# Causal attention in a fused vision kernel: the products for q as four tensor tiles of 32 rows by 32 columns

## The chip, the cores and the metric

The program runs on one NeuronCore of a Trainium2 chip. The metric is the device time of one execution in microseconds. The core has a matrix engine (PE, TensorE), a vector engine (DVE), a scalar engine (ACT), GpSimd (POOL) and queues of DMAs issued from SyncE (SP). Each engine takes its instructions in program order and waits on semaphores. Matmul results go to PSUM, which has eight banks of 512 float32 columns on each of 128 partitions.

## The reference, cut to what matters

Four layers follow each other on the same activations, 16 images of 56 x 56 = 3136 tokens with 32 channels: a window attention, two token MLPs, and twice (L2, L3) a causal attention over all 3136 tokens of an image with an expert-choice layer behind it. The change touches only the two causal attentions:

```
Q = embeddings @ W_Q
K = embeddings @ W_K
V = embeddings @ W_V
scores = jnp.einsum('bqd,bkd->bqk', Q, K) * scale
masked = jnp.where(causal[None, :, :], scores, -inf)
probs = jax.nn.softmax(masked, axis=-1)
return jnp.einsum('bqk,bkd->bqd', probs, V)
```

The kernel folds the weights together: with x the normalised tokens, the scores are x (W_Q W_K^T) x^T, so that one small matrix A (32 x 32) is enough. "q" below is A^T x^T, and the normalised tokens themselves serve as keys. What is computed and all sizes stay the same in the changed kernel.

## The kernel before, in words

`causal_attention` handles the images one after the other. Of each image it first makes VT (line 208, 32 channels of the transposed tokens, replicated four times over the 128 partitions, so that each group of 32 partitions holds a copy) and QT_ (line 209, the same for q). The replication has a purpose: a matmul that contracts over 32 channels uses only 32 rows of the array, and each copy feeds another group of 32 rows.

- **Scores** (line 404): keys on the output's partitions, 512 queries as columns. They are tiles of 32 rows by 128 columns and alternate between row groups 0 and 1 (`g0 = C * (n % 2)`, line 401). ACT takes the exponential from PSUM (line 529).
- **Maxima** (line 425): queries on the partitions, up to 512 keys as columns, in row groups 2 and 3 (line 422). DVE reduces each bank to one maximum for each query (line 561). The negated maxima go by DMA (line 289) into a row of QT_, as the channel that subtracts them from the scores.
- **pv** (line 502): exponentials times values, as four column tiles (128 rows by 32 columns), in batches of about 10 to 12 score banks; mask preloads (line 414), transposes that make VT (line 455) and the final product of a query block (lines 475 and 479) use all 128 rows.
- **q** (line 463): a stationary operand of 32 rows by 128 columns, A replicated four times (`A`, line 217), on row group 0, over 512 columns of VT (64 for the last of the seven blocks of an image). The result fills all 128 partitions of one bank, and ACT copies it to QT_ (line 546). An image has seven of these products; those of image i+1 stand within the work of image i.

Every float32 matmul appears in the trace as two passes, each with its own LDWEIGHTS and MATMUL. All work goes through one ring of eight PSUM banks (`RING`, line 80): `bank_free` (line 375) makes a matmul wait until ACT or DVE has read what was in the bank eight entries before. The order is a list `WORK` (line 172), sorted by a planned time and a rank, the same for all engines. It fixes where each q stands; scores and maxima go into the list mostly as two scores and two maxima in turn.

A line number with three forms (L404, L425, L502 and so on) names the same kind of work in both layers; the tiles are called L2a_... and L3a_.... In both the seven q of an image stand in the same places.

Of the kernel before, what the change touches and what calls it, by code (L numbers as in the profile page):

```python
# [21 lines left out]
C = 32  # L22
# [49 lines left out]
def causal_attention(nc, m, k, wq, wk, wv, eps, tag):  # L72

    NB = m.NB
    QB = 512
    NJ = -(-S // QB)
    QT = QB // P
# [5 lines left out]
    def rows(t):  # L83
        return P if t < LT else LAST
# [107 lines left out]
    with ExitStack() as ctx:  # L192
        def sb(name, shape, dt=F32):
            return ctx.enter_context(nc.sbuf_tensor(f"{tag}_{name}", shape, dt))
# [13 lines left out]
        VT = sb("vT", [P, 2, S])  # L208
# [8 lines left out]
        A = sb("A", [C, QT, C])  # L217
# [6 lines left out]
        def bank_of(x):  # L224
            if x[0] == "acc":
                x = ("pv", *x[1:])
            return R[PLACE[("mask", x[1]) if x[0] == "max" and x[1] in MASK_AT else x] % RING]
# [47 lines left out]
        item_full, item_copied, ot_ready = sem("item_full"), sem("item_copied"), sem("ot_ready")  # L275
        acc_copied, acc_added, rd_ready, t_added = sem("acc_copied"), sem("acc_added"), sem("rd_ready"), sem("t_added")

        with nc.Block() as block:
# [95 lines left out]
            def _(pe):  # L374
# [17 lines left out]
                for x in WORK:  # L392
                    kind = x[0]
                    if kind == "score":
                        n = x[1]
                        img, j, bank = SCORES[n]
                        bank_free(x)
                        if n == score_at(img, j):

                            pe.wait_ge(shift_in, shifts(img, j))  # L400
                        g0 = C * (n % 2)
                        for u, c0, c1, o in bank:
                            r = rows(u)
                            last = nc.tensor.matmul(bank_of(x)[0:r, o:o + c1 - c0],  # L404
                                                    VT[g0:g0 + C, img % 2, u * P:u * P + r],
                                                    QT_[g0:g0 + C, img % 2, j * QB + c0:j * QB + c1],
                                                    start=True, stop=True)
                        last.then_inc(s_full, 1)
                    elif kind == "mask":

                        _, j, _ = MAXES[x[1]]
                        bank_free(x)
                        mask = k.mask_qk[:][:, None, :].to_broadcast([P, QT, P]) if j < TAIL else k.mask_qk[:, P - LAST:P]
                        nc.tensor.matmul(bank_of(x)[:, 0:width(j)], k.ident_bf[:], mask, start=True, stop=False)
                    elif kind == "max":
                        n = x[1]
                        img, j, (part, d) = MAXES[n]
                        if n not in MASK_AT:
                            bank_free(x)
                        if n == max_at(img, j):  # L420
                            pe.wait_ge(item_copied, COPIED[("q", img, j)] + 1)
                        g0 = C * (2 + n % 2)

                        def dots(o, q0, c0, c1, start=True, stop=True):
                            return nc.tensor.matmul(bank_of(x)[:, o:o + c1 - c0], QT_[g0:g0 + C, img % 2, q0:q0 + P],  # L425
                                                    VT[g0:g0 + C, img % 2, c0:c1], start=start, stop=stop)

                        q0 = j * QB if j < TAIL else S - P
                        if part == "edge" and j < TAIL:

                            for i in range(QT):
                                last = dots(i * P, q0 + i * P, q0 + i * P, q0 + (i + 1) * P, False, i == QT - 1)
                        elif part == "edge":
                            last = dots(0, q0, LT * P, S, False)
                        elif part == "near":

                            if d == 0:
                                dots(0, q0 + P, q0, q0 + P)
                                last = dots(P, q0 + 3 * P, q0, q0 + 3 * P)
                            else:  # L440
                                last = dots(0, q0 + 2 * P, q0, q0 + 2 * P)
                        elif part == "far":
                            last = dots(0, q0 + d // j * P, d % j * QB, d % j * QB + QB)
                        else:
                            last = dots(0, q0, d * QB, d * QB + QB)
                        last.then_inc(m_full, 1)
                    elif kind == "vT":
                        _, img, f = x
                        bank_free(x)
                        if f == 0:  # L450
                            pe.wait_ge(vr_ready, img + 1)
                        for i in range(q_tiles(f)):
                            t = QT * f + i
                            r = rows(t)
                            last = nc.tensor.transpose(bank_of(x)[:, i * P:i * P + r],
                                                       VR[0:r, t].rearrange("p a c -> p (a c)"), k.ident[0:r, 0:r])
                        last.then_inc(item_full, 1)
                    elif kind == "q":
                        _, img, f = x
                        w = width(f)  # L460
                        bank_free(x)
                        pe.wait_ge(item_copied, COPIED[("vT", img, f)] + 1)
                        nc.tensor.matmul(bank_of(x)[:, 0:w], A[:].rearrange("p r c -> p (r c)"),
                                         VT[0:C, img % 2, f * QB:f * QB + w],
                                         start=True, stop=True).then_inc(item_full, 1)
                    elif kind == "final":
                        _, img, j = x
                        bank_free(x)
                        pe.wait_ge(acc_copied, FINAL[x] + 1)
                        added = [n for y, n in ADD.items() if y[:2] == (img, j)]  # L470
                        if added:
                            pe.wait_ge(acc_added, added[-1] + 1)
                        if j < TAIL:

                            nc.tensor.matmul(bank_of(x)[:, 0:QT * (C + 1)], O[:, FINAL[x] % 2],
                                             WFB[:].rearrange("p q c -> p (q c)"),
                                             start=True, stop=True).then_inc(item_full, 1)
                        else:
                            nc.tensor.matmul(bank_of(x)[0:LAST, 0:C + 1], O[:, FINAL[x] % 2, 0:LAST], WF[:],
                                             start=True, stop=True).then_inc(item_full, 1)  # L480
                    elif kind == "pv":
                        _, img, j, n0, n1 = x
                        bank = bank_of(x)
                        bank_free(x)
                        pe.wait_ge(exp_done, n1)
                        masked = [n for n in range(n0, n1) if n in MASK]
                        if masked:
                            pe.wait_ge(mask_done, MASK[masked[-1]] + 1)
                        if n0 == score_at(img, j):
                            pe.wait_ge(v_ready, img + 1)  # L490
                        order = [(u, c0) for n in range(n0, n1) for u, c0, *_ in SCORES[n][2]]
                        for n in range(n0, n1):
                            for u, c0, c1, o in SCORES[n][2]:
                                r = rows(u)

                                if j < TAIL:
                                    cuts = [(i, i * P - c0, (i + 1) * P - c0, [y for y, c in order if c <= i * P])
                                            for i in range(c0 // P, QT)]
                                else:
                                    cuts = [(u % 4, 0, LAST, [y for y, c in order if y % 4 == u % 4])]  # L500
                                for i, a, b, same in cuts:
                                    last = nc.tensor.matmul(bank[C * i:C * i + C, 0:b - a], V[0:r, img % 2, u, :],  # L502
                                                            E[0:r, n % RE, o + a:o + b],
                                                            start=u == same[0], stop=u == same[-1])
                            last.then_inc(pv_done, 1)
# [1454 lines left out]
```

## Time and profile before

| what | value |
|---|---|
| median of 2 runs | 4702.2 us (4697.58 to 4706.83) |
| the profiled execution: time | 4710.27 us |
| the profiled execution: span of its instructions | 4708.6 us |
| PE busy | 4141.0 us (88%), 51290 matmul passes |
| DVE busy | 3134.4 us (67%) |
| ACT busy | 2752.3 us (58%) |
| POOL busy | 1430.2 us (30%) |
| mean granted TensorE clock | 0.942 of 2.4 GHz |

The busy time of an engine is the union of its records. A record of a matmul starts when its weights begin to load or its columns begin to stream, and its end is modelled: it includes the way through the array. So several matmuls in different row groups lie above each other in the trace, and a PE that is "busy" may well have three of its four row groups free. The causal attentions take the stretches from 1550 to 2885 us (L2) and from 3130 to 4450 us (L3).

### The profile page before, as it was taken

The numbers are of one execution on the slowest core, as the hardware profiler recorded it, in microseconds if no ns is written. First come the engines' busy times: TensorE is split into PE (matmuls) and PEld (weight loads), VectorE is DVE, ScalarE is ACT, GpSimd is POOL, SyncE is SP. The second block draws the span as 40 slices with busy tenths as digits, with TensorE's granted clock in tenths as the row PEclk, the third lists the DMA queues.
The fourth block names the chain that finished last, engine by engine and source line by source line (L and its number), as shares of the span: only waits on it lengthen the run. The fifth ranks groups of instructions, "written<-read, shape, count | busy, mean of one in ns | idle before, by whom it ended". The sixth has DMA issues, their size and how long they took to land. (4 is left out here: it accounts for less than half of the span.)

```text
span 4708.6 us, 125775 instructions
## 1 busy us (share of the span) xinstructions
PE 4141.0 (88%) x51290; PEld 2867.8 (61%) x51290; DVE 3134.4 (67%) x6164; ACT 2752.3 (58%) x5706; POOL 1430.2 (30%) x2222
## 2 busy tenths in 40 slices
PE   3888888888686799999999999779999999999975
PEld 2666666666332466666676666456666666666754
DVE  4777777777798466666666666536666666666653
ACT  2777777776586355655655555415555556556541
POOL 4333223321000343433433432122433434334220
PEclk9999999999798699999999999769999999999987
DMA  1200000000000000000000000000000000000003
GB/s 25 33 3 3 2 2 3 2 2 2 3 1 1 1 2 2 2 2 3 2 3 2 2 2 2 6 1 2 2 2 2 3 2 2 2 2 2 3 6 55
DMA packets 348272, 24.07 MB, mean 5 GB/s; under 512 B 346388, under 2 KB 347700, under 8 KB 347700
## 3 DMA queue, kind: packets, MB, share of 16 engines
q1 hardware_dynamic: 347700, 16.03, 4.7%
q8 instruction: 409, 6.70, 0.6%
q14 instruction: 163, 1.34, 0.1%
HBM read 7.88 MB, written 6.42 MB: 3 GB/s over the span
## 5 line engine op out<-in xcount | busy, mean ns | idle before, releaser
L561 DVE TENSOR_REDUCE L2a_mx<-L2a_r 128x1 f32<-128x512 f32 (+4 forms) x1344 | 760.8, 627 | 243.4 <-PE L2a_r L425 240.3
L561 DVE TENSOR_REDUCE L3a_mx<-L3a_r 128x1 f32<-128x512 f32 (+4 forms) x1344 | 760.5, 627 | 239.8 <-PE L3a_r L425 236.4
L529 ACT ACTIVATE L2a_e<-L2a_r 128x512 f32<-128x512 f32 (+3 forms) x1344 | 658.8, 579 | 284.9 <-PE L2a_r L404 282.7
L529 ACT ACTIVATE L3a_e<-L3a_r 128x512 f32<-128x512 f32 (+3 forms) x1344 | 658.6, 579 | 280.5 <-PE L3a_r L404 278.5
L425 PE MATMUL L2a_r<-L2a_vT,L2a_qT 32*128 32x512 f32 (+3 forms) x3488 | 817.6, 529 | 0.0
L425 PE MATMUL L3a_r<-L3a_vT,L3a_qT 32*128 32x512 f32 (+3 forms) x3488 | 815.0, 528 | 0.1
L404 PE MATMUL L2a_r<-L2a_qT,L2a_vT 32*128 32x512 f32 (+4 forms) x3488 | 779.8, 518 | 29.4 <-DMA L2a_qT<-L2a_nm 29.4
L404 PE MATMUL L3a_r<-L3a_qT,L3a_vT 32*128 32x512 f32 (+4 forms) x3488 | 777.6, 516 | 27.3 <-DMA L3a_qT<-L3a_nm 27.3
L1454 POOL TENSOR_SCALAR win_xw<-win_xr,win_mv,win_rs 32x343 f32<-32x343 f32 (+7 forms) x432 | 327.9, 779 | 703.3 <-ACT win_rs L1242 703.2
L404 PEld LDWEIGHTS L2a_r<-L2a_qT,L2a_vT 32*128 32x128 f32 x3488 | 372.1, 188 | 189.3 <-issue 100.3
L404 PEld LDWEIGHTS L3a_r<-L3a_qT,L3a_vT 32*128 32x128 f32 x3488 | 370.6, 187 | 186.8 <-issue 98.9
L425 PEld LDWEIGHTS L2a_r<-L2a_vT,L2a_qT 32*128 32x128 f32 x3488 | 394.0, 194 | 51.0 <-DVE L2a_mx L561 24.3
L425 PEld LDWEIGHTS L3a_r<-L3a_vT,L3a_qT 32*128 32x128 f32 x3488 | 390.8, 192 | 51.0 <-DVE L3a_mx L561 25.0
L502 PEld LDWEIGHTS L2a_r<-L2a_e,L2a_v 128*32 128x32 f32 x10400 | 302.5, 111 | 118.9 <-ACT L2a_e L529 100.3
L502 PEld LDWEIGHTS L3a_r<-L3a_e,L3a_v 128*32 128x32 f32 x10400 | 302.3, 111 | 119.1 <-ACT L3a_e L529 100.3
L502 PE MATMUL L2a_r<-L2a_e,L2a_v 128*32 128x128 f32 x10400 | 347.1, 273 | 3.9 <-POOL L2a_e L363 3.1
L502 PE MATMUL L3a_r<-L3a_e,L3a_v 128*32 128x128 f32 x10400 | 346.5, 273 | 4.1 <-POOL L3a_e L363 3.3
L1106 PE MATMUL win_mx<-win_mk,win_xw 113*64 113x196 f32 x2048 | 202.7, 339 | 134.1 <-issue 126.5
L1268 ACT COPY win_yb<-win_yp 64x512 f32<-64x512 f32 x256 | 148.3, 579 | 237.5 <-PE win_yp L1190 236.0
L1220 ACT COPY win_mq<-win_pq 32x392 f32<-32x392 f32 x512 | 246.6, 482 | 57.3 <-PE win_pk L1099 50.1
L363 POOL TENSOR_SCALAR_AFFINE_SELECT L2a_e<-L2a_e 128x128 f32<-128x128 f32 (+2 forms) x304 | 98.8, 326 | 581.2 <-ACT L2a_e L529 567.5
L363 POOL TENSOR_SCALAR_AFFINE_SELECT L3a_e<-L3a_e 128x128 f32<-128x128 f32 (+2 forms) x304 | 98.8, 326 | 576.8 <-ACT L3a_e L529 563.0
(370 smaller groups left out, 6745.0 us busy)
## 6 DMA issues: line engine op xcount, KB each, us to landing
L2a_qT<-L2a_nm SPq DMA_DIRECT2D x768, 0.5 KB, 2.0
L3a_qT<-L3a_nm SPq DMA_DIRECT2D x768, 0.5 KB, 2.0
T<-in_x SPq DMA_DIRECT2D x16, 384.0 KB, 3.7
out<-T SPq DMA_DIRECT2D x16, 384.0 KB, 4.0
win_mq<-win_nmt SPq DMA_DIRECT2D x256, 3.1 KB, 1.7
win_msk<-in_L_conv_pos_emb SPq DMA_DIRECT2D x49, 0.2 KB
L2a_qT<-L2a_nm SPq DMA_DIRECT2D x32, 0.2 KB, 1.8
L3a_qT<-L3a_nm SPq DMA_DIRECT2D x32, 0.2 KB, 1.8
```

Of the source, the lines that this page charges most:

```text
L363: nc.gpsimd.affine_select(out=e, in_=e, compare_op=ALU.is_ge, fill=0.0, base=0, pattern=pattern, channel_multiplier=-1).then_inc(mask_done, 1)
L404: last = nc.tensor.matmul(bank_of(x)[0:r, o:o + c1 - c0], VT[g0:g0 + C, img % 2, u * P:u * P + r], QT_[g0:g0 + C, img % 2, j * QB + c0:j * ...
L425: return nc.tensor.matmul(bank_of(x)[:, o:o + c1 - c0], QT_[g0:g0 + C, img % 2, q0:q0 + P], VT[g0:g0 + C, img % 2, c0:c1], start=start, st ...
L502: last = nc.tensor.matmul(bank[C * i:C * i + C, 0:b - a], V[0:r, img % 2, u, :], E[0:r, n % RE, o + a:o + b], start=u == same[0], stop=u = ...
L529: nc.scalar.activation(E[0:r, n % RE, 0:w], bank_of(x)[0:r, 0:w], ACT.Exp).then_inc(exp_done, 1)
L561: return nc.vector.tensor_reduce(to, frm, AX.X, ALU.max)
L1106: last = nc.tensor.matmul(bank[half * SLOT:(half + 1) * SLOT, c0:c0 + HK], window(n, 2 * p + half), buf[:, slot, half, p].rearrange("p h c ...
L1220: last = nc.scalar.copy(MQ[0:C, q_slot(n), :, :, h, :], PQ[h * C:(h + 1) * C, 0:NW * K].rearrange("p (w f c) -> p f w c", f=2, c=K))
L1268: last = nc.scalar.copy(YB[r, n % 2, :, :, half, :].rearrange("p a h c -> p (a h) c"), YP[r, :].rearrange("p (a c) -> p a c", c=C))
L1454: last = nc.gpsimd.tensor_scalar(dst, s, MV[:, 0:1], RS[:], ALU.subtract, ALU.mult)
```

## The change

The q product is issued as four matmuls, one for each group of 32 output partitions, each with one copy of A (32 rows by 32 columns) as its stationary operand and the same 512 columns of VT. All four work on row group 0, each in its own group of 32 columns of the array. Everything else keeps its shape and its place.

```diff
@@ -460,9 +460,11 @@
                         w = width(f)
                         bank_free(x)
                         pe.wait_ge(item_copied, COPIED[("vT", img, f)] + 1)
-                        nc.tensor.matmul(bank_of(x)[:, 0:w], A[:].rearrange("p r c -> p (r c)"),
-                                         VT[0:C, img % 2, f * QB:f * QB + w],
-                                         start=True, stop=True).then_inc(item_full, 1)
+                        for g in range(QT):
+                            last = nc.tensor.matmul(bank_of(x)[g * C:g * C + C, 0:w], A[:, g],
+                                                    VT[0:C, img % 2, f * QB:f * QB + w],
+                                                    start=True, stop=True)
+                        last.then_inc(item_full, 1)
```

On PE, the place of the two q products that follow each other (block 1 and 2 of the next image), before. A row is a line, an operation, the tiles it writes and reads, and the output's partitions by columns:

```order
L404 MATMUL L2a_r7<-L2a_qT,L2a_vT 128x512
L425 MATMUL L2a_r0<-L2a_vT,L2a_qT 128x512
L425 MATMUL L2a_r1<-L2a_vT,L2a_qT 128x512
L463 MATMUL L2a_r2<-L2a_vT,L2a_A 128x512
L463 MATMUL L2a_r3<-L2a_vT,L2a_A 128x512
L404 MATMUL L2a_r4<-L2a_qT,L2a_vT 128x512
L404 MATMUL L2a_r5<-L2a_qT,L2a_vT 128x512
L425 MATMUL L2a_r6<-L2a_vT,L2a_qT 128x512
```

and the same place now:

```order
L404 MATMUL L2a_r7<-L2a_qT,L2a_vT 128x512
L425 MATMUL L2a_r0<-L2a_vT,L2a_qT 128x512
L425 MATMUL L2a_r1<-L2a_vT,L2a_qT 128x512
L464 MATMUL L2a_r2<-L2a_vT,L2a_A 32x512 x4
L464 MATMUL L2a_r3<-L2a_vT,L2a_A 32x512 x4
L404 MATMUL L2a_r4<-L2a_qT,L2a_vT 128x512
L404 MATMUL L2a_r5<-L2a_qT,L2a_vT 128x512
L425 MATMUL L2a_r6<-L2a_vT,L2a_qT 128x512
```

Nothing has moved: the q rows have become four tiles each, between maxima and scores that are unchanged. The second place is the q product ahead of a mask preload (line 414, 128 rows by 128 columns), on PE, before:

```order
L425 MATMUL L2a_r6<-L2a_vT,L2a_qT 128x512
L425 MATMUL L2a_r7<-L2a_vT,L2a_qT 128x512
L463 MATMUL L2a_r0<-L2a_vT,L2a_A 128x512
L414 MATMUL L2a_r1<-mask_qk,ident_bf 128x512
L404 MATMUL L2a_r2<-L2a_qT,L2a_vT 128x512
```

and now:

```order
L425 MATMUL L2a_r6<-L2a_vT,L2a_qT 128x512
L425 MATMUL L2a_r7<-L2a_vT,L2a_qT 128x512
L464 MATMUL L2a_r0<-L2a_vT,L2a_A 32x512 x4
L414 MATMUL L2a_r1<-mask_qk,ident_bf 128x512
L404 MATMUL L2a_r2<-L2a_qT,L2a_vT 128x512
```

Here too only the q row differs. In the whole program it is 224 such rows, and no row of another engine differs.

## Rows read from the trace of the kernel before

**Rows 1.** Busy time by engine in the two causal attentions (stretch, length, engines, PE's clock)

```profile
1550.00:2885.00 1335.00, 1284.25 (x16980) 898.89 (x16982) 858.97 (x1736) 757.95 (x1633) 488.41 (x801) 0.96 0.05 2
3130.00:4450.00 1320.00, 1279.44 (x16977) 893.14 (x16976) 859.52 (x1738) 757.33 (x1632) 478.08 (x793) 0.97 0.05 2
```

**Rows 2.** Waits from 1550 to 2885 us: total, times, longest

```profile
DVE L2a_mx L561 <- PE L2a_r L425: 233.5, 257, 24.7
```

**Rows 3.** Line 463: instructions, their count, duration and forms

```profile
L463 PE MATMUL L2a_r<-L2a_vT,L2a_A x224: 270/587/1218, 1561.1 to 2882.2; 32*128 32x512 f32 x96, 32*128 32x64 f32 x16
```

**Rows 4.** Timeline of PE: start, length, line, tile of the array, times; 32*64 before 32*128

```profile
2203.80 0.32 PE L404 MATMUL L2a_r<-L2a_qT,L2a_vT 32*64 32x64 f32 x2
2204.05 0.69 PE L425 MATMUL L2a_r<-L2a_vT,L2a_qT 32*128 32x512 f32 x1
```

**Rows 5.** Timeline of PE in the token MLPs: four column tiles of 512 columns

```profile
1331.94 1.06 PE L856 MATMUL mlp_u<-mlp_hs,mlp_w2a 128*32 128x512 f32 x8
1332.93 0.70 PE L844 MATMUL mlp_h<-mlp_xT,mlp_w1a 32*128 32x512 f32 x3
```

**Rows 6.** Timeline of PE at the q ahead of a pv batch (brackets: idle, what ended it)

```profile
2216.92 1.12 PE L463 MATMUL L2a_r<-L2a_vT,L2a_A 32*128 32x512 f32 x2 [0.82 <-DVE L2a_mx L561]
2217.97 0.32 PE L502 MATMUL L2a_r<-L2a_e,L2a_v 128*32 128x128 f32 x4
```

**Rows 7.** Timeline at the two q in a row: PE, then the next DVE start

```profile
2228.38 0.59 PE L425 MATMUL L2a_r<-L2a_vT,L2a_qT 32*128 32x512 f32 x2
2228.59 1.45 PE L463 MATMUL L2a_r<-L2a_vT,L2a_A 32*128 32x512 f32 x3
...
2229.88 0.59 PE L463 MATMUL L2a_r<-L2a_vT,L2a_A 32*128 32x512 f32 x1
...
2230.73 0.59 PE L404 MATMUL L2a_r<-L2a_qT,L2a_vT 32*128 32x512 f32 x1
...
2231.44 0.69 DVE L561 TENSOR_REDUCE L2a_mx<-L2a_r 128x1 f32<-128x512 f32 x1 [0.77 <-PE L2a_r L425]
```

**Rows 8.** Timeline at the q between maxima and scores before a batch: PE, then DVE

```profile
2239.89 1.11 PE L425 MATMUL L2a_r<-L2a_vT,L2a_qT 32*128 32x512 f32 x3
2240.49 0.69 PE L463 MATMUL L2a_r<-L2a_vT,L2a_A 32*128 32x512 f32 x1
...
2242.40 0.32 PE L502 MATMUL L2a_r<-L2a_e,L2a_v 128*32 128x128 f32 x4
...
2242.59 0.69 DVE L561 TENSOR_REDUCE L2a_mx<-L2a_r 128x1 f32<-128x512 f32 x1 [0.36 <-PE L2a_r L425]
```

**Rows 9.** Timeline at the q in mid-stretch: PE, then the DVE start it reaches

```profile
2253.42 0.59 PE L425 MATMUL L2a_r<-L2a_vT,L2a_qT 32*128 32x512 f32 x2
...
2255.73 0.69 DVE L561 TENSOR_REDUCE L2a_mx<-L2a_r 128x1 f32<-128x512 f32 x1
```

**Rows 10.** Timeline at the q ahead of the mask preload: PE, then DVE

```profile
2264.61 0.66 PE L404 MATMUL L2a_r<-L2a_qT,L2a_vT 32*128 32x512 f32 x1 [1.30 <-DMA L2a_qT<-L2a_nm]
...
2265.15 0.59 PE L425 MATMUL L2a_r<-L2a_vT,L2a_qT 32*128 32x512 f32 x2
...
2265.76 0.39 PE L414 MATMUL L2a_r<-mask_qk,ident_bf 128*128 128x512 bf16 x1
...
2267.44 0.69 DVE L561 TENSOR_REDUCE L2a_mx<-L2a_r 128x4 f32<-128x512 f32 x1 [0.17 <-PE L2a_r L425]
```

**Rows 11.** Timeline at the q of 64 columns: PE, then DVE's next idle time

```profile
2275.15 0.48 PE L425 MATMUL L2a_r<-L2a_vT,L2a_qT 32*128 32x384 f32 x1
...
2278.46 0.69 DVE L561 TENSOR_REDUCE L2a_mx<-L2a_r 128x1 f32<-128x512 f32 x1 [0.28 <-PE L2a_r L425]
```

**Rows 12.** Busy time by engine in two images, and in the first image's lead

```profile
2132.30:2216.90 84.60, 82.67 (x1146) 58.48 (x1146) 56.75 (x116) 50.43 (x110) 32.58 (x55) 1.00 0.05 2
1784.20:1872.60 88.40, 85.78 (x1146) 59.97 (x1146) 56.75 (x116) 50.47 (x110) 32.59 (x55) 0.96 0.05 2
...
1561.00:1597.00 36.00, 36.00 (x121) 19.37 (x123) 15.59 (x32) 5.98 (x12) 8.05 (x13) 0.50 0.05 1
```

## The prediction

> **What bounds the kernel now.** I read the busy time by stretch first. In the two causal attentions PE shows 1284 of 1335 us and 1279 of 1320 us, DVE 859 and ACT 758 of the same stretches [rows 1]. That looks like a kernel bound by PE alone, but a busy PE here means that at least one of its four row groups works. So the timeline has to say what each engine waits for. DVE waited 257 times for maxima of line 425, 233.5 us in total in the first attention, 24.7 us of it once, at the start [rows 2]. Read over one image, the timeline shows two phases that alternate. In a stretch of scores and maxima DVE works back to back, 0.69 us for each maximum by its record [rows 7], a little less from start to start, and PE waits for banks that DVE frees. In a pv batch, a transpose or a wait for the shift DMA, DVE runs dry and waits for PE. The chain that sets the end runs through both. A delay of PE is therefore lost time where DVE has nothing queued, and is partly hidden where DVE has up to four finished maxima in the ring. Each place of a q has to be costed by itself.
>
> **What the change removes and adds.** It removes 112 products of 32 x 128 in each layer, two passes each: 224 passes in the trace, of 270 to 1218 ns, for 96 products of 512 and 16 of 64 columns in each layer [rows 3], where the counts of the shapes are of one pass in two. It adds four tiles of 32 x 32 for each. The columns that stream stay 512, so the product itself doesn't get shorter if the four tiles run side by side; what changes is the weight load, and the shape of tile that PE is in.
>
> The trace has no 32 x 32 tile between 32 x 128 ones, but it has the nearest shapes. First, four column tiles of 512 columns, 128 rows high: the set starts at 1331.94 and the next shape at 1332.93, so **a set of four costs 0.99 us** alone, passes, loads and turn-round together [rows 5]. One 32 x 128 product alone starts at 2216.92 and hands over to the next shape at 2217.97: 1.05 us [rows 6]. The tiles are thus 0.06 us shorter than the single product where both stand alone. Were the four tiles to take turns, a set would cost about 3.6 us (eight passes of 0.43 us, which is a quarter of the way through the two q in rows 7: four pass starts, three steps in 1.29 us).
>
> Second, the turn-round. When PE goes from 32*64 to 32*128, with the same 32 rows, the next record starts at 2204.05, while the one before ends by the model at 2203.80 + 0.32 = 2204.12 [rows 4]. It is 0.07 us before the end. Where the shape stays, the next record starts far before the end: at 2239.89 + 1.11 = 2241.00 the maxima end, and the q of the same shape had started at 2240.49 [rows 8]. So a change of the columns alone makes PE wait until all row groups have run out. **I take it that each set of q tiles waits for all scores and maxima before it, and that all behind it wait for the set.** Until now q blocked one row group of four, and the rest streamed on.
>
> The Trainium skill says this too, under "TensorEngine Tiling (Array Packing)", Tiling Modes, Key Properties: changing the tiling mode, not just the tile, drains TensorE. The trace agrees (0.07 us before the modelled end). By that rule the places below are delayed; were there no drain, the sum would be -18 us at most (first rival).
>
> **The six places of an image, by the rows** (a foursome of scores and maxima from free row groups takes 1.05 us to the next shape and 1.12 us to its end, as the q in rows 6 did):
>
> - *Ahead of a pv batch* [rows 6]: PE stands idle 0.82 us before it and changes its shape behind it anyway. 0.99 instead of 1.05: **-0.06**.
> - *Two q in a row* [rows 7]: the maxima before end at 2228.38 + 0.59 = 2228.97, the set can start at 2228.90. The first costs 0.99, the second 0.86 more (two passes of 0.43), so scores and maxima start again at 2230.75 and end at 2231.87. Before, the score that had waited behind q in row group 0 ended at 2230.73 + 0.59 = 2231.32, and DVE, dry for 0.77 us, started at 2231.44. **+0.55**.
> - *Between maxima and scores, just before a batch* [rows 8]: maxima end at 2241.00, so q from 2240.93, the foursome behind it from 2241.92, pv from 2242.97 instead of 2242.40. DVE is dry there too (0.36). **+0.57**.
> - *In mid-stretch* [rows 9]: maxima end at 2254.01, q from 2253.94, foursome from 2254.93 to 2256.05, DVE at about 2256.13 instead of 2255.73. The maxima already queued hide the rest. **+0.40**.
> - *Ahead of the mask preload* [rows 10]: now q runs beside a score and two maxima that end at 2265.74. Then q would start at 2265.67 and the mask preload at 2266.66 instead of 2265.76. The maximum behind it found DVE dry at 2267.44. All is lost: **+0.90**.
> - *The q of 64 columns* [rows 11]: it waits for maxima until 2275.15 + 0.48 - 0.07 = 2275.56 and takes some 0.2 us, but DVE has queued work until 2278.2. **+0.05** (0 to 0.4).
>
> The sum is 2.41 us for an image. The places come again to within 0.01 us in the images that I compared, and 15 images in each of two layers have them: **+72 us**.
>
> The q of each layer's first image stand in the lead-in, where PE runs at a granted clock of 0.50, 1.2 GHz [rows 12], so that a set costs twice 0.99. Some stand beside changes of shape anyway. I take five places at 1 us in each layer: **+10 us** (0 to 20).
>
> **The clock.** An image of 84.6 us had the clock at 1.00, one of 88.4 us at 0.96 [rows 12]: 2 x 0.04 x 88.4 = 7 us of it passed at 1.2 GHz, in two short drops, so a drop costs up to (88.4 - 84.6) / 2 = 1.9 us. I take 1.6, since images without a drop are not all equally long. The drops that I found follow the places of rows 6 and rows 10, where PE idles and then has q alone or nearly alone. With the change q is alone in three places more, two of them with no idle time of PE beside them. I guess eight more drops in thirty images: 8 x 1.6 = **+13 us** (between -10, if places shift away from the drops, and +48, one more in each image).
>
> **Other engines.** ACT copies q from the same bank in one instruction as before. DMAs are unchanged. The bank of q and its four quadrants are filled by one set, and one semaphore increment stands on the last tile. The 1344 more instructions (six passes more for each of 224, each with its load) are hidden: rows 5 is a set of the same eight passes, loads and all, in 0.99 us, of which the columns stream for 0.86 us.
>
> Sum: 4710 + 72 + 10 + 13 = 4805 us for the profiled execution, which lies 8 us above the median of the runs. Against the median: 4702 + 95 = **4797 us**.
>
> **Rivals.**
> 1. *No drain between shapes of 32 rows.* Each tile goes into row group 0 as q did, with a load of 32 instead of 128 columns, 0.06 to 0.08 us less. 224 x 0.08 = 18 us at most, most of it not on the chain: 4684 to 4702, not slower. It decides at whether the first record of a set starts while maxima still stream. Against it speaks rows 4, a change of columns at equal rows. The Trainium skill's "TensorE: Matmul & The Clock Gate", Part 3, tells of row and column tiles that run side by side, all of one shape; no row here shows unlike ones side by side. Chance 0.04.
> 2. *The tiles of one row group take turns.* 3.6 instead of 0.99 us for 192 sets: +500 us, 5290. Against it: rows 5 and the pv tiles, four at a time from the same partitions. Chance 0.03.
> 3. *DVE's queue hides more.* If half of the four large places are absorbed, +36 + 10 + 5: about 4753. DVE's waits of 0.77, 0.36 and 0.17 us at three of them speak against it. Chance 0.09.
> 4. *The clock falls in nearly each image at a new place,* and the lead-in costs its upper bound: 72 + 20 + 48 = +140, 4842. Chance 0.09.
>
> **How the numbers follow.** The forecast itself, +60 to +130 us, has 0.75. A difference of 2%, 94 us, is about what a measurement of this kernel can tell from no change, and the forecast lies on it, so I split it in two. Slower by over 2%: half of it, and rivals 2 and 4: 0.50. Within 2%: the other half, rival 3 and most of rival 1: 0.48. Faster by over 2%: 0.02. The range goes from near rival 3 to rival 4: 4757 to 4842.
>
> **What would show it.** In the profile of the changed kernel line 464 must appear with 32*32, four records within some 0.02 us, from 0.07 us before the last maximum's end, and the next score 0.99 us later. In an image, DVE's wait at the two q should grow from 0.77 to about 1.3 us and at the mask preload from 0.17 to about 1.1; an image should take 2.4 us more at a clock of 1.00. The prediction is wrong if a score or maximum streams beside a set, if the set is longer than 1.1 us, or if images without a drop of the clock are longer by less than 1.2 or more than 3.5 us.

## The result

The changed kernel takes 4836.3 us (median of 2 runs, 4834.5 to 4838.1) where the kernel before takes 4702.2 us: 134 us more, a ratio of 1.0285 with a 95% interval of 1.0239 to 1.0332. It is slower. The forecast was 4797 us in a range of 4757 to 4842 us: the direction and the range hold, and the size was 39 us short.

The page of the profile after, engines first. PE has 52634 matmul passes instead of 51290, the 1344 more that the four tiles bring, and 126 us more busy time; DVE and ACT are busy for as long as before.

```profile
span 4832.8 us, 128463 instructions
...
PE 4267.1 (88%) x52634; PEld 2803.6 (58%) x52634; DVE 3138.4 (65%) x6164; ACT 2763.6 (57%) x5706; POOL 1430.1 (30%) x2222
```

Line 464, which is line 463 of before [rows 3], has 896 passes in each layer (the counts behind the shapes are of a sample), at 32*32:

```profile
L464 PE MATMUL L2a_r<-L2a_vT,L2a_A x896: 214/587/1058, 1561.1 to 2946.8; 32*32 32x512 f32 x154, 32*32 32x64 f32 x26
```

**Where the time went, by stretch.** In each layer 14 image periods are alike: from the 64-query product at the end of image 0 to that of image 14. Of these 28 periods the profile before and after gives (stretch, length, busy time of PE, its weight loads, DVE, ACT and POOL, the granted clock, DMA):

```profile
1700.20:2910.10 1209.90, 1173.03 (x16039) 826.62 (x16038) 794.87 (x1610) 705.38 (x1522) 442.43 (x742) 0.98 0.05 2
3269.20:4474.10 1204.90, 1169.75 (x16040) 823.81 (x16040) 794.81 (x1610) 705.02 (x1522) 442.48 (x742) 0.99 0.05 2
```

```profile
1712.40:2974.40 1262.00, 1228.05 (x16622) 800.94 (x16621) 796.35 (x1610) 710.90 (x1522) 442.39 (x742) 0.96 0.05 2
3337.50:4597.50 1260.00, 1222.70 (x16621) 799.39 (x16620) 796.36 (x1610) 710.73 (x1522) 442.48 (x742) 0.97 0.05 2
```

They took 2414.8 us and take 2522.0: +107 us, 3.8 us for each image. The other 17 us of the span's +124 lie in the lead-ins, which hold the first image's own six places too, and in the last images. The clock column (1.00 is 2.4 GHz, 0.50 is 1.2 GHz) explains a part. From the unrounded record of the clock, 75 us of the 28 periods passed at 1.2 GHz before, and 184 us now. A straight line through the 28 pairs of period and time at 1.2 GHz gives 85.1 us + 0.42 us for each such microsecond before, and 87.2 us + 0.44 us now. So 2.1 us an image, 59 us in all, are there at full clock, and (184 - 75) x 0.44 = 48 us come from the clock. The 87.2 us are extrapolated, since no period of the changed kernel is without time at 1.2 GHz.

**The places, after.** At the two q in a row [rows 7] the four-tile sets stand alone, 16 passes between the end of the maxima and the start of the next scores, and DVE waits 1.33 us instead of 0.77:

```profile
2174.68 0.59 PE L425 MATMUL L2a_r<-L2a_vT,L2a_qT 32*128 32x512 f32 x2
2175.21 1.92 PE L464 MATMUL L2a_r<-L2a_vT,L2a_A 32*32 32x512 f32 x16
2177.05 0.70 PE L404 MATMUL L2a_r<-L2a_qT,L2a_vT 32*128 32x512 f32 x2
...
2178.30 0.69 DVE L563 TENSOR_REDUCE L2a_mx<-L2a_r 128x1 f32<-128x512 f32 x1 [1.33 <-PE L2a_r L425]
```

The maxima end at 2174.68 + 0.59 = 2175.27 and the set starts at 2175.21; it ends at 2177.13 and the scores start at 2177.05. Nothing else of PE lies between. It is so for all 224 sets of the trace: no other matmul of PE overlaps one of them by more than 0.07 us. Before, scores and maxima of the other row groups started while q streamed. At the single q just before a batch [rows 8] it is the same with one set: 0.99 us from its start to that of the scores, and DVE waits 0.93 instead of 0.36 us.

```profile
2187.78 1.06 PE L464 MATMUL L2a_r<-L2a_vT,L2a_A 32*32 32x512 f32 x8
2188.77 0.70 PE L404 MATMUL L2a_r<-L2a_qT,L2a_vT 32*128 32x512 f32 x2
...
2190.02 0.69 DVE L563 TENSOR_REDUCE L2a_mx<-L2a_r 128x1 f32<-128x512 f32 x1 [0.93 <-PE L2a_r L425]
```

In mid-stretch [rows 9] DVE worked through before; now it waits 0.47 us. Ahead of a pv batch [rows 6] the set takes 0.99 us where the single product took 1.05:

```profile
2203.63 0.69 DVE L563 TENSOR_REDUCE L2a_mx<-L2a_r 128x1 f32<-128x512 f32 x1 [0.47 <-PE L2a_r L425]
```

```profile
2164.22 1.06 PE L464 MATMUL L2a_r<-L2a_vT,L2a_A 32*32 32x512 f32 x8 [0.82 <-DVE L2a_mx L563]
2165.21 0.32 PE L504 MATMUL L2a_r<-L2a_e,L2a_v 128*32 128x128 f32 x4
```

Ahead of the mask preload [rows 10] the picture is another one. The records are longer, because the clock is at 1.2 GHz: the set takes 2217.11 - 2215.25 = 1.86 us instead of 0.99. The stretch at 0.50 lasts 10.3 us here.

```profile
2213.24 1.19 PE L404 MATMUL L2a_r<-L2a_qT,L2a_vT 32*128 32x512 f32 x1 [2.03 <-DMA L2a_qT<-L2a_nm]
...
2215.25 1.93 PE L464 MATMUL L2a_r<-L2a_vT,L2a_A 32*32 32x512 f32 x8
2217.11 0.61 PE L414 MATMUL L2a_r<-mask_qk,ident_bf 128*128 128x512 bf16 x1
```

```profile
2212.40:2222.70 10.30, 9.46 (x51) 5.37 (x53) 3.54 (x9) 3.79 (x8) 0.08 (x1) 0.50 0.01 0
```

In the 28 images the clock fell at this place 10 times before, for 3.4 us each (34 us). Now it falls there in all 28, for 3.4 to 10.2 us (184 us). The 12 other falls of before (41 us), 1.4 to 2.5 us behind the start of block 0, in the pv batch or at the 64-query product, are gone. So all of the time at 1.2 GHz in the periods is at this one place, and the falls have become 28 instead of 22, but of 6.6 us on average instead of 3.4. In the lines above the clock fell at 2212.4, ahead of the set; in 13 of the 28 images it was down before the set began, in 15 it fell later.

### The profile page after: what moved, and what is told of

It reads as the page before. It is cut to its first block and busy times, and to the rows that moved or that the text cites. A ratio compares the mean times of both kernels' runs of the same rounds, so it can differ in the third digit from the quotient of the medians.

```text
span 4832.8 us, 128463 instructions
## 1 busy us (share of the span) xinstructions
PE 4267.1 (88%) x52634; PEld 2803.6 (58%) x52634; DVE 3138.4 (65%) x6164; ACT 2763.6 (57%) x5706; POOL 1430.1 (30%) x2222
## 5 line engine op out<-in xcount | busy, mean ns | idle before, releaser
L404 PE MATMUL L3a_r<-L3a_qT,L3a_vT 32*128 32x512 f32 (+4 forms) x3488 | 762.0, 526 | 28.8 <-DMA L3a_qT<-L3a_nm 28.8
L404 PE MATMUL L2a_r<-L2a_qT,L2a_vT 32*128 32x512 f32 (+4 forms) x3488 | 762.6, 526 | 26.2 <-DMA L2a_qT<-L2a_nm 26.2
L404 PEld LDWEIGHTS L3a_r<-L3a_qT,L3a_vT 32*128 32x128 f32 x3488 | 363.2, 191 | 232.2 <-issue 104.3
L404 PEld LDWEIGHTS L2a_r<-L2a_qT,L2a_vT 32*128 32x128 f32 x3488 | 362.6, 191 | 227.9 <-issue 101.3
```

What stands on the lines that cost most here:

```text
L404: last = nc.tensor.matmul(bank_of(x)[0:r, o:o + c1 - c0], VT[g0:g0 + C, img % 2, u * P:u * P + r], QT_[g0:g0 + C, img % 2, j * QB + c0:j * ...
```

## The experiments

The question was whether the 59 us are the waits for a change of shape, as forecast, and what makes the clock fall: any q that runs alone, the 32 x 32 tiles as such, or this one q behind the wait for the shift DMA. Twelve kernels ran; each ratio is against runs of the kernel before on the same chip. "At 1.2 GHz" is the time in the 28 image periods, 75 us in the kernel before and 184 us in the changed one.

| kernel | median us | ratio (95% interval) | 28 periods us | of it at 1.2 GHz us | images of 28 in which the clock falls at block 5 |
|---|---|---|---|---|---|
| before | 4702.2 | 1 | 2414.8 | 75 | 10 |
| after | 4836.3 | 1.0285 (1.0239 to 1.0332) | 2522.0 | 184 | 28 |
| e1, only the q ahead of the mask tiled | 4804.8 | 1.0192 (1.0167 to 1.0216) | 2491.1 | 225 | 28 |
| e2, all but that one tiled | 4771.9 | 1.0124 (1.0102 to 1.0146) | 2456.0 | 85 | 20 |
| e3, two tiles of 32 x 64 | 4853.2 | 1.0291 (1.0268 to 1.0314) | 2542.0 | 229 | 28 |
| e4, 32 x 128, odd blocks in row group 1 | 4763.7 | 1.0094 (1.0074 to 1.0114) | 2477.0 | 212 | 28 |
| e5, only block 1 in row group 1 | 4704.2 | 0.9986 (0.9977 to 0.9996) | 2417.3 | 122 | 21 |
| e6, only block 5 in row group 1 | 4795.5 | 1.0175 (1.0155 to 1.0195) | 2497.7 | 239 | 28 |
| e7, only block 0 tiled | 4707.8 | 0.9992 (0.9983 to 1.0001) | 2402.1 | 65 | 10 |
| e8, as after, block 5 one step later | 4884.7 | 1.0371 (1.0352 to 1.0390) | 2557.6 | 270 | 23 |
| e9, e5 and block 5 one step later | 4705.6 | 0.9988 (0.9978 to 0.9998) | 2420.4 | 140 | 24 |
| e10, as after, block 5 one step earlier | 4772.4 | 1.0130 (1.0110 to 1.0150) | 2454.3 | 92 | 15 |
| e11, e5 and block 5 one step earlier | 4696.2 | 0.9967 (0.9953 to 0.9981) | 2406.5 | 109 | 22 |
| e12, e11 and block 0 tiled | 4699.0 | 0.9971 (0.9958 to 0.9984) | 2394.7 | 89 | 16 |

The kernel before had medians of 4711 to 4715 us in these later runs, so ratios, not medians, are to be compared. The periods, the time at 1.2 GHz and the falls are of one profiled execution each. Block 5 is issued as before in e2, e5 and e7 too, and there the clock falls at it in 20, 21 and 10 images, so that a difference of some ten images between two of these kernels may be chance. The mean granted clock is on record for every run, and 2 x (1 - clock) x span is a run's time at 1.2 GHz. By medians over runs, that is more than in the kernel before on the same chip by 164 us in e1, 26 in e2, 138 in e3, 102 in e4, 18 in e5, 154 in e6, 226 in e8, 37 in e9, 22 in e10 and 12 in e12, and less by 10 in e7 and 2 in e11; a step of 0.001 in the clock is 9 us.

### e1 and e2: one place against the other six

The loop of the change, for block 5 alone (e1); e2 has `f != 5` in its first line.

```diff
+                        parts = 4 if f == 5 else 1
+                        n = P // parts
+                        for g in range(parts):
+                            last = nc.tensor.matmul(bank_of(x)[g * n:g * n + n, 0:w],
+                                                    A[:].rearrange("p r c -> p (r c)")[:, g * n:g * n + n],
+                                                    VT[0:C, img % 2, f * QB:f * QB + w],
+                                                    start=True, stop=True)
+                        last.then_inc(item_full, 1)
```

> Only the q ahead of the mask preload (block 5 of each image) is issued as four 32 x 32 tiles, the other six stay 32 x 128. Theory 1 (this q brings the lost clock): it adds about 0.9 us for each image by the wait for the maxima, and every image gets a drop to 1.2 GHz at this place, some 6 us at 1.2 GHz for each image instead of 2.7: (0.9 + 3.3 x 0.44) x 30 = +70 us, 4772. Theory 2 (the clock falls from q being alone anywhere): 0.9 x 30 plus a seventh to a quarter of the clock's 50 us: +35 to +40 us, 4740, and fewer than half of the images with a drop at this place.

> All q are four 32 x 32 tiles except the one ahead of the mask preload. Theory 1 (the clock is lost by that one): the time at 1.2 GHz stays near 2.7 us for each image, and the places add 0.55 + 0.57 + 0.45 - 0.06 = 1.5 us for each image: +45 us and some 8 for the lead-in, 4755. Theory 2 (the clock is lost anywhere): the same 53 us and 35 to 45 us more, 4790 to 4800.

Measured: 1.0192 and 1.0124. With the kernel before at 4702 us that is +90 and +58 us, which sums to 148 us, near the 134 us of the change. Of e1's 28 periods 225 us are at 1.2 GHz, of e2's 85 us. The clock column of the two, e1 first:

```profile
1704.50:2953.90 1249.40, 1214.84 (x16123) 841.62 (x16122) 796.19 (x1610) 709.59 (x1522) 443.48 (x742) 0.95 0.05 2
```

```profile
1710.30:2938.90 1228.60, 1194.26 (x16538) 791.71 (x16537) 795.43 (x1610) 708.75 (x1522) 443.47 (x742) 0.98 0.05 2
```

So one q of seven makes nearly two thirds of the loss, and nearly all of the lost clock, as theory 1 had it (its +70 us were measured as +90); the expected 53 us of the other six were measured as 58. In e2, the distances of DVE's maxima at full clock grow by 0.55 us (two in a row), 0.57 (before a batch) and 0.45 us (mid-stretch) and shrink by 0.06 us (ahead of pv), to the hundredth the same as in the changed kernel; all other distances from one maximum to the next, outside the place of the mask preload, stay within 0.04 us. That is the sum of the forecast, place by place.

### e3: columns, not number of tiles

The same loop with `parts = 2`: two tiles of 32 rows by 64 columns.

> All q as two tiles of 32 rows by 64 columns instead of four of 32 by 32. Theory of the drain (any other number of columns makes PE wait until all row groups have run out): as slow as the changed kernel, 4825 to 4845 us, and 0.03 us more for each weight load of 64 columns. Rival (the cost comes from the number of tiles and passes, eight loads and eight matmuls instead of two): half of the loss or less, 4770 or below.

Measured: 1.0291 against 1.0285. At the two q in a row the set is again alone, and DVE waits as long as in the changed kernel:

```profile
2270.66 1.93 PE L466 MATMUL L2a_r<-L2a_vT,L2a_A 32*64 32x512 f32 x8
2272.52 0.70 PE L404 MATMUL L2a_r<-L2a_qT,L2a_vT 32*128 32x512 f32 x2
...
2273.76 0.69 DVE L566 TENSOR_REDUCE L2a_mx<-L2a_r 128x1 f32<-128x512 f32 x1 [1.34 <-PE L2a_r L425]
```

Half the passes, the same 1.93 us and the same loss: it isn't the number of instructions. The drain comes with 64 columns as with 32, between neighbours of 128.

### e4: what one row group costs

Here q keeps its shape; A has a second copy on partitions 32 to 63, and odd blocks use row group 1:

```diff
-        A = sb("A", [C, QT, C])
+        A = sb("A", [2 * C, QT, C])
...
+                        g0 = C * (f % 2)
-                        nc.tensor.matmul(bank_of(x)[:, 0:w], A[:].rearrange("p r c -> p (r c)"),
-                                         VT[0:C, img % 2, f * QB:f * QB + w],
+                        nc.tensor.matmul(bank_of(x)[:, 0:w], A[g0:g0 + C].rearrange("p r c -> p (r c)"),
+                                         VT[g0:g0 + C, img % 2, f * QB:f * QB + w],
```

> The q keep their shape of 32 x 128, but blocks 1, 3 and 5 use row group 1 (A has a second copy on partitions 32 to 63), so that the two q in a row run side by side. If what q costs before is that it holds one row group, and that the score queued behind the second q in row group 0 ends last, DVE's wait of 0.77 us there goes: 0.7 to 0.85 us less for each image, -20 to -25 us, 4678. If PE's row groups are not what is waited for, no change within 5 us.

Measured: 1.0094, slower, where 0.5% faster was expected. The mechanism was there: at the two q in a row DVE's distance shrank by 0.39 us. But 212 us of the 28 periods were at 1.2 GHz. Block 5, the q ahead of the mask preload, had moved into the row group in which the score just before it ran, so that it started behind that score and ended alone. That was not meant, and it gave the next two experiments.

### e5 and e6: the two effects of e4 apart

The same kernel with `g0 = C * (f == 1)` (e5) and `g0 = C * (f == 5)` (e6). e6 has no tile of another shape anywhere.

> Shapes of before; only block 1 of each image uses row group 1, so that the two q in a row run side by side, and all others stay in row group 0. In the run with blocks 1, 3 and 5 in row group 1 this place gave back 0.39 us for each image, but the q ahead of the mask preload stood alone behind a score of the same row group and the clock fell there in each of 28 images. Theory: without that the clock falls as rarely as before and the 0.39 us are kept: -12 us, 4691 (0.25% faster). Rival (any change of row groups lets the clock fall more): slower than before, like the earlier run.

> Shapes of before, no change of shape at all; only block 5, the q ahead of the mask preload, uses row group 1, in which the score just before it runs. Theory: what costs at this place is that q runs alone behind a wait for a DMA, whether a change of shape or a taken row group makes it so: 0.8 us for each image and a drop of the clock in each, +70 to +90 us, as the run with only this q tiled (4805). Rival (the 32 x 32 tiles themselves let the clock fall): 0.8 x 30 = +24 us, and the clock as before.

e6 is the strongest result here: 1.0175, nearly the 1.0192 of e1, with 239 us at 1.2 GHz, and no change of shape. Its timeline at the place:

```profile
2198.22 0.59 PE L405 MATMUL L2a_r<-L2a_qT,L2a_vT 32*128 32x512 f32 x1
2198.25 0.59 PE L426 MATMUL L2a_r<-L2a_vT,L2a_qT 32*128 32x512 f32 x2
2198.64 1.56 PE L465 MATMUL L2a_r<-L2a_vT,L2a_A 32*128 32x512 f32 x2
2200.14 0.61 PE L415 MATMUL L2a_r<-mask_qk,ident_bf 128*128 128x512 bf16 x1
```

```profile
2199.00:2205.80 6.80, 6.80 (x39) 4.63 (x39) 3.49 (x9) 3.67 (x9) 0.16 (x1) 0.50 0.01 0
```

Score and maxima are out by 2198.84, q runs on until 2200.20, and the clock is at 1.2 GHz from 2199.0 for 6.8 us. So a 32 x 32 tile isn't what the clock reacts to. In all five kernels in which a q has PE to itself behind the idle time of this place (the changed one, e1, e3, e4 and e6), the clock falls there in every image. That q alone doesn't trigger each fall: in 18 of the 28 images of e6, and in 18 of e1, the clock was at 1.2 GHz before q began. What brings it down there stays open. The rival, +24 us and the clock as before, falls.

e5 keeps the 0.39 us. DVE waits 0.39 us instead of 0.77:

```profile
2232.07 0.69 DVE L563 TENSOR_REDUCE L2a_mx<-L2a_r 128x1 f32<-128x512 f32 x1 [0.39 <-PE L2a_r L426]
```

It is faster by 0.14% (0.04 to 0.23%), about 7 us instead of the expected 12. Its time at 1.2 GHz is 122 instead of 75 us, which fits a part of the gain given back to the clock. Over all runs the clock gives 18 us more at 1.2 GHz, which is two steps of its last digit, so that this isn't shown.

### e8 and e9: block 5 one step later

```diff
-            timed += [(at, ("vT", img, f)), (at + 4, ("q", img, f))]
+            timed += [(at, ("vT", img, f)), (at + (6 if img and f == 5 else 4), ("q", img, f))]
```

e8 has this in the changed kernel, e9 in e5.

> The changed kernel, all q as 32 x 32 tiles, but block 5 is planned one step later, behind the mask preload and the scores and maxima that follow the wait for the shift DMA. Theory: idle time of PE and a q alone are then apart, the clock falls no more often than before; the drains stay, some 0.5 us for this place: 2.0 us for each image and 8 to 15 us for the lead-in, 4770 to 4780, 55 to 65 us less than the changed kernel. Rival (the tiles cost that clock wherever they stand): 4820 or more.

> Shapes of before, block 1 in row group 1, and block 5 one step later as in the run before this one. Theory: 12 us from the two q side by side; the q moved away from the wait is in nobody's way where it stands now, and the clock falls at most as often: 4670 to 4690. Rival: the later q delays scores of row group 0 by up to 0.4 us for each image and gives the 12 us back.

e8 came out at 1.0371, the slowest of all: the theory that idle time and a lone q only have to be kept apart falls. The rival (4820 or more) holds here, but e10 below answers its "wherever they stand". 23 of the 28 images have the clock at 1.2 GHz there, for 6.8 to 13.7 us:

```profile
2217.91 0.66 PE L404 MATMUL L2a_r<-L2a_qT,L2a_vT 32*128 32x512 f32 x1 [1.85 <-DMA L2a_qT<-L2a_nm]
...
2219.37 0.61 PE L414 MATMUL L2a_r<-mask_qk,ident_bf 128*128 128x512 bf16 x1
...
2222.94 1.93 PE L464 MATMUL L2a_r<-L2a_vT,L2a_A 32*32 32x512 f32 x8
2224.80 1.22 PE L404 MATMUL L2a_r<-L2a_qT,L2a_vT 32*128 32x512 f32 x2
```

The mask preload at 2219.37 has a record of 0.61 us, the length that it has at 1.2 GHz (0.39 in [rows 10]), so the clock was down before the set began. The set then ran alone for 1.86 us at the low clock, and the clock stayed down. So it was in all 23: the fall came 1.8 to 5.7 us ahead of the set. Five images in which it never fell took 86.5 to 86.7 us, as little as the drains alone explain. In e9, with q 32 x 128 at the same later place beside scores and maxima, the clock fell in 24 images, as often as in e8, but for 3.4 or 6.8 us, 120 us at this place where e8 has 249. What the pair supports is this: where the clock is down, a q alone keeps it down. e9 is at 0.9988, as fast as e5, which on 4702 us is 4696 and not the expected 4670 to 4690.

### e10 and e11: block 5 one step earlier

The same line with `2` for `6`. The q now stands ahead of the scores that wait for the shift DMA.

> The changed kernel, all q as 32 x 32 tiles, but block 5 is planned one step earlier, ahead of the wait for the shift DMA (1.30 us of idle PE) instead of behind it. Theory A (the drain costs time only where it isn't hidden, and the clock falls from a q alone that comes after the idle time): the set of 0.99 us lies in the wait, the 0.9 us of this place are gone, and the idle time is short enough that the clock falls rarely: 1.5 us for each image and 8 to 15 us for the lead-in, 4755 to 4765. Rival B (idle time and a q alone add up in whichever order they come): 4755 and 30 to 45 us for the clock, 4790 to 4805.

> Shapes of before, block 1 in row group 1 (0.39 us less for each image, 0.14% faster as measured), and block 5 one step earlier, in the wait for the shift DMA. By theory A the clock now has four groups at work at once behind the wait and no q: it falls less often at this place, up to 15 us less than the run with block 1 alone: 4685 to 4695. By rival B nothing changes against that run: 4700 to 4705.

e10: 1.0130, on the kernel before's 4702 us that is 4763 us, in the range of theory A, and 73 us below the changed kernel with all its 32 x 32 tiles in place. The set lies in the wait:

```profile
2283.01 1.06 PE L464 MATMUL L2a_r<-L2a_vT,L2a_A 32*32 32x512 f32 x8
2284.00 1.88 PE L404 MATMUL L2a_r<-L2a_qT,L2a_vT 32*128 32x512 f32 x3
2285.22 0.70 PE L425 MATMUL L2a_r<-L2a_vT,L2a_qT 32*128 32x512 f32 x2
...
2286.69 0.61 PE L414 MATMUL L2a_r<-mask_qk,ident_bf 128*128 128x512 bf16 x1
```

92 us are at 1.2 GHz, near the 75 of before. The lone q ahead of the wait costs next to nothing, the same q behind it costs its drain and the clock. The order isn't tested by itself, though, since the set and the score behind it fill the idle time: the longest that PE is idle at this place is 0.5 us by the median of the images, 1.9 us in the changed kernel. Rival B's 4790 to 4805 us were missed, but that idle time of the same length ahead of or behind a lone q would differ isn't shown.

e11 is the fastest of the study by its ratio, 0.9967 (0.9953 to 0.9981), 15 us below the kernel before. Against e5 it is 0.2% faster, about what was expected of it, but the intervals of the two overlap a little. Its reason isn't shown: over all runs it has less time at 1.2 GHz than e5 (2 us below the kernel before instead of 18 above), but in the profiled execution the clock fell at this place in 22 images, in e5 in 21.

### e7 and e12: the one place where the tiles cost nothing

e7 has `parts = 4 if f == 0 else 1`, e12 the same on top of e11.

> Only block 0 of each image, the q that stands alone ahead of a pv batch, is tiled 32 x 32; the other six stay 32 x 128. The forecast has -0.06 us for each image here, since the change of shape is only moved from behind q to ahead of it, where PE is idle: -2 us, no measurable change, 4700 to 4705. Rival (any set of tiles costs 0.2 us and more, for loads and turn-round): +6 us or more for the places, and more if the clock falls at this place.

> The three edits that each gave something or nothing, together: block 1 in row group 1, block 5 one step earlier, and block 0, alone ahead of a pv batch, as 32 x 32 tiles. If they add up: 0.33% from the first two and 0.04 to 0.08% from the third, ratio 0.9955 to 0.9965, some 16 to 20 us below the kernel before. If the third does nothing: 0.9967 as without it.

e7 is at 0.9992 (0.9983 to 1.0001): no change that could be measured, with DVE's distance at the place 0.06 us shorter. The rival, +6 us and more, falls. e12 at 0.9971 (0.9958 to 0.9984) is as fast as e11; whether the tiled block 0 adds its 0.06 us there can't be told.

## Why the prediction was right, and where it was short

- **The drain between shapes of unequal columns** [rows 4]: right. Each set starts 0.06 us before the modelled end of the maxima (2175.27 to 2175.21), and the scores start 0.08 us before the end of the set. e3 shows it for 64 columns too. No other matmul overlaps a set by more than that. The Trainium skill's rule that a change of tiling mode drains TensorE ("TensorEngine Tiling (Array Packing)", Tiling Modes, Key Properties) holds for a change of columns alone.
- **A set of four costs 0.99 us** ([rows 5], 128 rows high): right for 32 rows too, 0.99 us in three places. The tiles of one row group don't take turns, so rival 2 is out; the second of two sets took 0.86 us as forecast (2175.21 to 2177.05 is 1.84).
- **The places**, forecast and measured by DVE's distances at full clock: two in a row +0.55 and +0.55, before a batch +0.57 and +0.57, mid-stretch +0.40 and +0.45, ahead of pv -0.06 and -0.06. The q of 64 columns: no distance behind it moved by more than 0.04 us, +0.05 forecast.
- **Ahead of the mask preload, +0.90**: as a delay of PE right, as a loss of time not confirmed. In eight images the clock fell only at the end of the set or behind it. There the mask preload starts 2.06 us (2.10 in one) behind the first score after the wait, before the change 1.15 us: 0.91 us. How much of it reaches the end is known only roughly, since no image has the maxima behind it at full clock. The 59 us at full clock less 28 x 1.51 us of the other places leave 17 us, 0.6 us an image. e1, with this place alone, is 76 us longer in its periods, of which (225 - 75) x 0.44 = 66 us are the clock: 0.4 us an image. Against e10, which takes the set out of this place, it is 68 - (184 - 92) x 0.44 = 28 us, 1.0 us an image, but e10 also gains over the kernel before here: its images without a fall take 86.4 us where 85.2 + 1.5 would be 86.7. So "all is lost" is the step that none of this bears out, and 0.4 to 0.6 us is the better reading.
- **The sum of the places, +72 us for thirty images**: 59 us in 28 periods at full clock is 63 in thirty. A little less than forecast, and the difference is about that of the mask preload.
- **The clock, +13 us**: this was the term that was mis-sized. It was 48 us in the 28 periods. Eight more falls of 1.6 us each were guessed in thirty images. There are six more in 28, 28 instead of 22, so that the number was near, by luck, as it was a guess over all places; what was missing is that a fall gets longer, 6.6 us on average instead of 3.4, where a q alone follows. Six falls of the old length would have been 9 us. And they are all in one place. The mechanism of a lone q next to idle time was named, but with the wrong weight: it isn't enough that q is alone (at two in a row it has PE alone for 1.84 us, with no idle time before, and the clock didn't fall there), nor that PE idles before (10 to 21 of 28 images in the kernels with block 5 as before). With both, the clock fell 28 times in 28, though in 13 of them ahead of the set. Rival 4, 4842 us, was the nearest in number and had 0.09; it had the falls at a new place, and they are at one where the clock had fallen before.
- **The range** held by 6 us, 4836 in 4757 to 4842, because its upper end was rival 4. Of the span's 124 us, 59 are the places in the 28 periods (28 x 2.41 = 67 forecast), 48 the clock (13), and 17 the lead-ins and last images (10, and 5 for two images more).
- **The lead-in, +10**: it can't be separated from the first image's own six places; both and the last images together are 17 us of the span.

## What to carry to other kernels

In this kernel a small product between matmuls that share the array by row groups was best left in exactly their tile shape. A tile with fewer columns is no cheaper here, since as many columns stream through it (0.99 us for a set of four, 1.05 us for the single product), and it takes all of the array for that time instead of a quarter. If such a product has to differ, put it where PE changes its shape anyway (e7, no loss), or ahead of a wait that it can fill (e10, 1.3% slower instead of 2.9%), not behind one. And look at a timeline for places where PE idles and then has little to do: of the 76 us that e1's periods are longer, about 10 are the delay of the lone q, and 66 the clock.

## What was not expected of the hardware

- The clock's reaction depends on the order of a handful of neighbouring instructions. The same set of tiles left 184 us at 1.2 GHz behind the wait for a DMA, 92 us ahead of it, and 270 us a step later. Why e8's clock falls in 23 images, before the set has begun, isn't settled. That q no longer fills the fourth row group behind the wait isn't shown to be the reason: in e5 and e2 it does, and the clock falls in 21 and 20 images, and in e9 and e11 it doesn't, in 24 and 22.
- Scores and maxima in free row groups ran past a q, but were reported in program order. In the kernel before, the first of the two maxima behind the two q ended by its record at 2230.07 + 0.59 = 2230.66:

```profile
2230.07 0.59 PE L425 MATMUL L2a_r<-L2a_vT,L2a_qT 32*128 32x512 f32 x1
```

  DVE started on it at 2231.44 only [rows 7]. The trace has the semaphores of the four products raised in the order of the program, the two scores' at 2231.34 and 2231.38 and the two maxima's at 2231.42 and 2231.46, all after the score in row group 0, behind the two q, had ended at 2231.32. One q in another row group gave 0.39 us of that back (e5).
